# Two value products in place of three for the second pair of steps of each key tile

## The reference

```python
q = (x @ Wq + bq).reshape(B, T, 8, 128); kv = x @ Wkv + bkv
k, v = kv[..., :128], kv[..., 128:]
q = q + pe; k = k + pe
scores = einsum('bhqd,bkd->bhqk', q, k) / sqrt(128)     # causal mask
attn = einsum('bhqk,bkd->bhqd', softmax(scores), v)
out = attn.reshape(B, T, 1024) @ Wo
```

## Time and profile before

| | us |
|---|---|
| median of 3 runs | 1515.31 |
| lowest and highest | 1510.8, 1518.69 |
| span of the profiled execution, first to last instruction | 1512.0 |

### The profile page before, as it was taken

How to read it: one execution, slowest core, us unless ns; L and a number is a source line. 1 busy time by engine, 2 the same in 40 slices (tenths; PEclk the granted TensorE clock), 3 DMA queues, 4 the chain that set the end, 5 groups by cost and what they waited for, 6 DMA issues and landing times.

```text
span 1512.0 us, 36188 instructions
## 1 busy us (share of the span) xinstructions
PE 1484.7 (98%) x11724; PEld 1448.2 (96%) x11724; DVE 1262.6 (84%) x3424; ACT 1052.6 (70%) x2531; POOL 1153.7 (76%) x1665
## 2 busy tenths in 40 slices
PE   7999999999999999999999999999999999999998
PEld 6999999999999999999999999999999999999998
DVE  7988869888698896988879888788887988879875
ACT  5777667776677766767677676767767776777764
POOL 6787777787777787877778777778777787778774
PEclk9999999999999999999999999999999999999999
DMA  4144422444224542344423444134441344413453
GB/s 129 44 126 135 132 87 67 116 141 141 74 69 119 146 137 60 86 120 139 128 58 96 120 137 136 43 100 122 137 139 38 105 130 138 138 29 101 127 153 105
DMA packets 225801, 164.39 MB, mean 109 GB/s; under 512 B 51792, under 2 KB 220880, under 8 KB 225616
## 3 DMA queue, kind: packets, MB, share of 16 engines
q1 hardware_dynamic: 224768, 161.69, 37.1%
q10 hardware_dynamic: 848, 0.40, 0.1%
HBM read 81.27 MB, written 77.59 MB: 105 GB/s over the span
## 4 chain that ended last, share of the span: by engine, by line
PE 75%; DVE 10%; DMA 7%; SPq 3%; issue 3%; ACT 1%; POOL 1%; DVEq 0%; ACTq 0%; POOLq 0%
PE pS L1036 26%; PE pO L1173 21%; PE pG L1036 12%; PE pG L1123 8%; PE pT L1139 7%; DMA park_dram<-Y 5%; SPq L455 3%; DVE X L1015 2%; DVE mix L861 1%; DMA Z<-park_dram 1%; DVE Y L924 1%; DVE pt L940 1%; DVE qtmp L850 1%; PE pS L1123 1%; DVE xn L810 1%
## 5 line engine op out<-in xcount | busy, mean ns | idle before, releaser
L766 ACT ACTIVATE X<-X,bias 128x16 f32<-128x16 f32 (+56 forms) x512 | 376.0, 734 | 156.3 <-DVE bias L1015 154.8
L1036 PE MATMUL pS<-kt,qt 128*128 128x288 f32 (+41 forms) x2304 | 462.2, 329 | 4.1 <-DVE kv L837 2.5
L1173 PE MATMUL pO<-pt,v 128*128 128x256 f32 x3288 | 435.4, 283 | 2.5 <-DVE ot L994 2.4
L1173 PEld LDWEIGHTS pO<-pt,v 128*128 128x128 f32 x3288 | 399.8, 189 | 3.6 <-DVE ot L994 3.4
L575 POOL TENSOR_SCALAR X<-X,rec 128x16 f32<-128x16 f32 (+56 forms) x512 | 373.6, 730 | 26.9 <-DVE rec L914 16.2
L1015 DVE CUSTOM_DVE_ANT_0 X<-pS,mask 128x16 f32<-128x16 f32 (+56 forms) x512 | 353.7, 691 | 40.8 <-PE pS L1036 33.9
L1036 PEld LDWEIGHTS pS<-kt,qt 128*128 128x128 f32 x2304 | 365.2, 189 | 16.8 <-issue 3.7
L542 POOL TENSOR_TENSOR pt<-Z,pt 128x256 fp32r<-128x256 f32 (+5 forms) x192 | 317.7, 1655 | 78.7 <-ACT pt L688 77.8
L527 POOL TENSOR_TENSOR qt<-qtmp,qt 128x256 fp32r<-128x256 f32 x252 | 194.5, 772 | 62.8 <-ACT qt L661 55.2
L940 DVE TENSOR_TENSOR pt<-pT,pt 128x512 fp32r<-128x512 f32 (+3 forms) x440 | 207.7, 493 | 37.9 <-ACT pt L695 37.1
L759 ACT CAST ot<-pO 128x256 fp32r<-128x256 f32 x256 | 95.9, 375 | 173.4 <-PE pO L1173 94.3
(11 more groups left out here) (118 smaller groups left out, 1943.4 us busy)
## 6 DMA issues: line engine op xcount, KB each, us to landing
park_dram<-Y SPq DMA_DIRECT2D x32, 512.0 KB, 2.6
Z<-park_dram SPq DMA_DIRECT2D x128, 128.0 KB, 3.0
park_dram<-Y SPq DMA_DIRECT2D x32, 448.0 KB, 3.2
Z<-park_dram SPq DMA_DIRECT2D x128, 112.0 KB, 2.7
park_dram<-Y SPq DMA_DIRECT2D x32, 384.0 KB, 2.9
Z<-park_dram SPq DMA_DIRECT2D x128, 96.0 KB, 2.5
park_dram<-Y SPq DMA_DIRECT2D x32, 320.0 KB, 2.9
Z<-park_dram SPq DMA_DIRECT2D x128, 80.0 KB, 2.2
```

The costliest lines, as they stand in the source:

```text
L766: nc.scalar.activation(x_row(s, 0, w), x_row(s, 0, w), ACT.Exp, bias=bias[:, j:j + 1], scale=-1.0, accum_out=total[:, j:j + 1]).then_inc(e ...
L1036: last = nc.tensor.matmul(out, a[i], m[j], start=start and k == 0, stop=stop and k == n - 1)
L1173: last = nc.tensor.matmul(pO[:, 0:2 * P], v[i][:, k, :], pt[j][:, pair % 2, k, :], start=n == 0, stop=n == 3 * nk - 1)
```

## The change

Pairs with `s % 8` of 2 and 3 (from step 8 on) end at most 64 positions into their last key tile. They are now `doubled`: POOL copies the probabilities of that tile once (`copies` is 2, so each copy has 64 rows after the transposition), and a new tile `vd` holds the high values of the tile's first 64 keys above the low values of the same keys. For that key tile PE runs two matmuls in place of three: value high by probability low over 64 rows (`rows`), and `vd` by the doubled high probabilities over 128 rows. `double` on SP loads `vd` by two DMAs from `v` for each key tile from 1 to 7, in turn `8 r + 5`, between `stack` and `fetch`. The low parts (L940, L542) are computed over all 128 rows as before. The clearing by POOL is rewritten for all kinds of steps; for steps that are not doubled it does what it did. ACT's `v_out` waits for the loads of `vd` before it overwrites `v`.

```diff
+def doubled(s):
+    return s >= H and 2 <= s % H < 4
+def span(s):
+    return 2 * SUB if packed(s) else 4 * SUB if doubled(s) else P
+def own(s):
+    return (s % H + 1) * SUB
+def copied(s):
+    return packed(s) or doubled(s)
...
-N_FIRST = [sum((SUB * 2 if packed(r) else P) > (r % H + 1) * SUB for r in range(s))
-           + sum((not scaled_by_act(r)) + packed(r) for r in range(s)) for s in range(STEPS + 1)]
+N_FIRST = [sum((span(r) > own(r)) + (not scaled_by_act(r)) + copied(r) for r in range(s)) for s in range(STEPS + 1)]
...
+        vd = sb("vd", [P, D], R)
...
+            def double(b, r):
+
+                sp.wait_ge(v_ready, b * NC + r // TPC + 1)
+                before = b * NT + (r - 1 if r > 1 else -1)
+                if before > 0:
+                    sp.wait_ge(pv_done, before * PAIRS + 2)
+                for i in range(2):
+                    sp.dma_start(vd[64 * i:64 * (i + 1), :].bitcast(F), v[i][0:64, r, :].bitcast(F)).then_inc(vd_loaded, 16)
+
             for b, it in turns():
                 if it < STEPS and it % PER == (2 if it >= PER else 11):
                     stack(b, it // PER)
+                if H <= it < STEPS and it % H == 5:
+                    double(b, it // H)
...
-                    if packed(s):
-                        own = (s % H + 1) * SUB
-                        last = x_row(s, s // H * P, (s // H + 1) * P).rearrange("p (i n) -> p i n", i=4)
-                        if own < 2 * SUB:
-                            nc.gpsimd.memset(last[:, :, own:2 * SUB], 0.0).then_inc(normed, 1)
-                        nc.gpsimd.tensor_scalar(last[:, 1:4, 0:own], last[:, 0:1, 0:own].broadcast_to((P, 3, own)),
+                    copies = P // span(s)
+                    last = x_row(s, s // H * P, (s // H + 1) * P).rearrange("p (i n) -> p i n", i=copies)
+                    if own(s) < span(s):
+                        nc.gpsimd.memset(last[:, :, own(s):span(s)], 0.0).then_inc(normed, 1)
+                    if copied(s):
+                        nc.gpsimd.tensor_scalar(last[:, 1:copies, 0:own(s)],
+                                                last[:, 0:1, 0:own(s)].broadcast_to((P, copies - 1, own(s))),
                                                 rec[:, j:j + 1], 1.0, ALU.mult, ALU.mult).then_inc(normed, 1)
                         pool.wait_ge(normed, b * N_BODY + N_FIRST[s + 1] - 1)
-                    elif zeroed(s):
-                        nc.gpsimd.memset(x_row(s, w, w + zeroed(s)), 0.0).then_inc(normed, 1)
...
-                    act.wait_ge(vs_loaded, 48 * (chunk_no(b, c) - NC + 1))
+                    n = chunk_no(b, c) - NC
+                    act.wait_ge(vs_loaded, 48 * (n + 1))
+                    act.wait_ge(vd_loaded, 32 * (n // NC * (NT - 1) + (n % NC + 1) * TPC - 1))
...
-                    plain = nk - packed(2 * pair)
-                    work = [(k, i, j) for i, j in ((0, 0), (1, 0), (0, 1)) for k in range(plain)]
+                    plain = nk - copied(2 * pair)
+                    work = [(k, i, j, P) for i, j in ((0, 0), (1, 0), (0, 1)) for k in range(plain)]
+                    if doubled(2 * pair):
+                        work.append((nk - 1, 0, 1, 4 * SUB))
...
-                        last = nc.tensor.matmul(pO[:, 0:2 * P], v[i][:, k, :], pt[j][:, pair % 2, k, :],
+                        last = nc.tensor.matmul(pO[:, 0:2 * P], v[i][0:rows, k, :], pt[j][0:rows, pair % 2, k, :],
                                                 start=n == 0, stop=n == 3 * nk - 1)
...
+                        if doubled(2 * pair):
+                            pe.wait_ge(vd_loaded, 32 * (b * (NT - 1) + part // H))
+                            last = nc.tensor.matmul(pO[:, 0:2 * P], vd[:, :], pt[0][:, pair % 2, nk - 1, :],
+                                                    start=False, stop=True)
```

More of the change, by code:

```diff
@@ L115, in packed @@
     return s >= H and s % H < 2
-def zeroed(s):
-    return P - (s % H + 1) * SUB
+def doubled(s):
[6 more added lines that the diff above has]
+    return packed(s) or doubled(s)
 def turned_before(s):
@@ L136, in scaled_by_act @@
 def scaled_by_act(s):
-    return not packed(s) and (s > 999)
+    return not copied(s) and (s > 999)
 def width(s):
@@ L318, in build @@
         vs_loaded = sem("vs_loaded")
+        vd_loaded = sem("vd_loaded")
         within_lo = sem("within_lo")
@@ L1151, in turn @@
                     nk = part // H + 1
-                    plain = nk - packed(2 * pair)
-                    work = [(k, i, j) for i, j in ((0, 0), (1, 0), (0, 1)) for k in range(plain)]
+                    plain = nk - copied(2 * pair)
+                    work = [(k, i, j, P) for i, j in ((0, 0), (1, 0), (0, 1)) for k in range(plain)]
+                    if doubled(2 * pair):
+                        work.append((nk - 1, 0, 1, 4 * SUB))
                     early = len(work) // 2 if nk > 8 else 0
                     for n in range(early, len(work)) if part % 2 else range(early):
-                        k, i, j = work[n]
+                        k, i, j, rows = work[n]
                         if n == 0:
```

## The result

The changed kernel takes 1538.3 us (1535.4 to 1539.3) against 1513.9 us of the kernel before in the same comparison: a ratio of 1.0152, 95% interval 1.0122 to 1.0182, that is 18 to 28 us. Forecast were 1518.0 us and a range up to 1531. The profiled execution has a span of 1533.7 us, 21.7 us more than before.

A forecast was written before the change was run, and what follows sets the result against it. PE was taken to bound the kernel, with a second path through SP's late fetches level up to turn 41. Saved matmuls -3.7 and loads +4.0 to 8.8 gave middle +2.7, on 1515.3: 1518.0 us, range 1509 to 1531.

The forecast's parts named there:

- The 64-row matmul: PE, doubled key tile: a 64-row matmul among 128-row ones keeps the 0.117 us pace, extra cost taken as 0.
- upper end of 2 x 166 ns: PE around the 64-row matmul: 166 ns at each of two steps if the array has to run empty.
- Rival 3: PE at the 64-row matmul: array runs empty at each row-count change, 1528.6 to 1536.6 us, say 1529; chance 0.30.
- The loads: SP, two DMAs of `vd` per key tile before a parking: later fetches, longer waits in turn 41, 4.0 to 8.8 us.
- it moves by only 0.1 to 0.4 us: DVE's L832 before step 32's scores and XT: how much later it starts when step 24's fetch is late.
- The copies: POOL, doubled pairs: 0.64 us more a pair, covered by idle time around turn 32; taken as 0, up to 5.1 us.
- The saved matmuls: PE, one matmul less in each of 56 doubled pairs: 3.7 us gained, 6.6 if PE's waits give way.

The follow-up runs named there:

- rows_alone: Kernel before, with the last three-fold product of the same 56 pairs reading 64 rows in place of 128: 1534.0 us, ratio 1.0129.
- rows_96: Kernel before, with the last three-fold product of the same 56 pairs reading 96 rows in place of 128: 1515.1 us, ratio 0.9995.
- vd_twice: Changed kernel, with the low-probability product of doubled pairs also using `vd` over 128 rows, so no 64-row matmul: 1524.3 us, ratio 1.0061.
- behind_park: vd_twice with the loads of `vd` moved in SP's list from before the parking of their turn to behind it: 1510.2 us, ratio 0.9962.

## Why the prediction was wrong

*The 64-row matmul: the step that failed.* "I take 0" was wrong: the runs show 0.39 us a pair and 17 to 22 us in all (rows_alone). The upper end of 2 x 166 ns was low as well. The reason given, that blocks keep the pace whatever tile they read, rested on rows of one kind only; every matmul there had 128 rows. The rule of the Trainium skill (TensorEngine Tiling (Array Packing), Key Properties), that a change of the tiling mode drains TensorE, stood against it. The runs agree with it in what they can show: three in a row cost what one does, and 96 rows, which its list of configurations doesn't have, cost nothing. That the array runs empty is not seen itself. Rival 3 had the place and the condition, a change of the row count, though rows_96 shows that not every change costs. Its times were 1529 to 1537 us, with a chance of 0.30; measured is 1538. That its upper end comes so near is in part luck, since both of its terms were too small (18.6 for the rows, 2.7 for the rest) and the parts don't simply add up, as said below.

*The loads: right place, size too small.* 4.0 to 8.8 us were forecast, 8.8 to 14.2 measured. The length on SP was right (1.15 us). What fell short is "it moves by only 0.1 to 0.4 us": I followed L688 of step 24 over `kt` alone and left out that the late fetch also holds up POOL's low part, and so `mh` and FK in turn 32. And the wait behind step 32 came to stand in turn 40, at `gate`, not only in turn 41. (One reading was off as well: single waits reach 1.3 us in the earlier trace rows, not 0.8. No term rests on it.)

*The copies.* Taken as 0, bounded at 5.1; measured 0.2 to 3.5 us. The stretch was the right one: turn 32.

*The saved matmuls.* 3.7 us taken, 6.6 as the other end. From the parts: loads 11.5 (0.0076 x 1515.9), copies 1.8, less 9.2 for vd_twice, leaves 4.1. From behind_park: 5.8 gained with the copies on board leave 7.6. The parts needn't add up exactly, as they share the waits of turns 32 to 42. Both are compatible with 3.7 to 6.6 within the intervals. Which it is stays open.

*The sum.* 18.5 to 21.8 for the rows, 11.5 for the loads, 1.8 for the copies, less 4 for the matmuls are 28 to 31 us; measured are 24.4, with an interval of 18 to 28. The single costs are thus somewhat more than the whole. Part of the 64-row matmul's cost takes the place of FK's wait, which the loads and the copies had made longer; that this is all of the missing part isn't shown.

*The range.* It ended at 1531 since it counted only the pairs behind turn 41 for rival 3. rows_alone speaks against that: the 32 pairs behind turn 41 make 12.5 us of 56 x 0.39 = 21.8, and 17 to 22 were measured. The waits up to turn 41 took up little of the rest. And the prediction's own full price for rival 3 was 1536.6, outside the range that it gave.

## What to carry to other kernels

Where a stream has 128-row matmuls, price a 64-row one as two changes and not as one matmul: before a 128-row product is cut to the 64 rows that it needs, look for an operand that makes the other 64 count (here `vd` a second time) or leave zeros in them. An in-order DMA queue that waits for its own transfer has free room behind the issue and none ahead of it: the same two DMAs cost 14 us more ahead of a parking than behind it. When a transfer gets later, follow every reader of its data to PE, not the one on the chain, and when a change brings in a form of instruction that no row shows, ask what its bound would do to the sign before taking it at nothing.

## What the runs showed of the hardware

- Going from 128-row to 64-row matmuls and back takes 0.37 to 0.39 us in this stream, in parts of about 0.09 us before the 64-row matmul, 0.2 behind it and 0.1 behind the next. A run of three 64-row matmuls costs the same (1533.6 and 1534.0 us), and 96 rows cost nothing (ratio 0.9995). A matmul and its weight load change their rows together here, so the runs don't tell which of the two makes the delay.
- A load of 64 rows of 512 bytes within SBUF holds SP for 0.58 us of issue, the 1.15 us of two, more than the 0.43 us of a fetch of 64 KB.
